# A two-layer decoder on one core: five norm tiles on GpSimd and three on VectorE, three heads' parts in flight in the last output projection, and the first key operands of the first cross-attention loaded one stage earlier

## The reference, cut to what matters

```
def _layernorm(x):  m, v = mean(x), var(x);  return (x - m) / sqrt(v + 1e-5)

layer 0:  x += self_attention(norm(x))                 # 16 heads of 32, with RoPE
          x += cross_attention(norm(x), ctx)           # 16 heads of 32; x and the weights wq, wp are
                                                       # rounded to int8 steps per row; k, v = ctx @ wkv.T + b
          x += experts(norm(x))                        # 8 experts, best 2 of them
layer 1:  x += self_attention(norm(x))
          x += cross_attention(norm(x), ctx)           # 16 heads of 128, 257 image rows apart
          x += experts(norm(x))                        # 32 experts, best 6, and shared ones
```

## Time and profile before

| what | value |
|---|---|
| median of 3 runs | 3031.25 us (3029.53 to 3034.3) |
| profiled execution, its own time | 3030.65 us |
| its span in the trace | 3028.9 us |
| TensorE busy | 2720.8 us, 90% of the span |
| mean granted TensorE clock | 0.943 of full speed |

### The profile page before, as it was taken

One profiled execution on the slowest core, in us unless ns is written; L12 is line 12 of the kernel. 1 busy time (PEld: TensorE's weight loads), 2 busy tenths in 40 slices (PEclk: granted clock), 3 DMA queues, 4 the chain that ended last, 5 costly groups with the idle time before them and its releaser, 6 DMA issues. The chain is left out here.

```text
span 3028.9 us, 47591 instructions
## 1 busy us (share of the span) xinstructions
PE 2720.8 (90%) x15710; PEld 1997.4 (66%) x15710; DVE 1479.3 (49%) x2648; ACT 1297.8 (43%) x2923; POOL 1139.0 (38%) x1037
## 2 busy tenths in 40 slices
PE   7887898996599498889999989999999879999997
PEld 5653443443588375568888879999987547777762
DVE  5575436766211427588875346767663341111115
ACT  2462524554111136466653248888872202222220
POOL 2352225666111206335554545555551302122116
PEclk9899999998699799999999999999999789999998
DMA  2332424310499414156667754444431129999987
GB/s 94 78 90 90 155 86 101 70 33 20 150 323 320 151 42 100 28 196 237 236 245 222 225 200 176 183 183 183 176 122 59 48 89 339 333 345 344 336 267 213
DMA packets 318192, 521.87 MB, mean 172 GB/s; under 512 B 35538, under 2 KB 168530, under 8 KB 309876
## 3 DMA queue, kind: packets, MB, share of 16 engines
q1 hardware_dynamic: 290100, 450.00, 46.1%
q0 software_dynamic: 13280, 43.53, 4.5%
q10 hardware_dynamic: 14688, 26.75, 2.5%
HBM read 365.39 MB, written 129.50 MB: 163 GB/s over the span
## 5 line engine op out<-in xcount | busy, mean ns | idle before, releaser
L1841 PE MATMUL ps<-moe_blocks_xgt,moe_blocks_w 128*128 128x128 f32 (+1 forms) x3000 | 357.9, 278 | 6.8 <-DMA moe_blocks_b1s<-rb_cols 3.4
L1841 PEld LDWEIGHTS ps<-moe_blocks_xgt,moe_blocks_w 128*128 128x128 f32 (+1 forms) x3000 | 342.8, 185 | 14.6 <-issue 8.5
L2804 POOL TENSOR_TENSOR normed<-normed,xa_core_rinv 128x257 f32<-128x257 f32 (+1 forms) x256 | 260.4, 1039 | 213.9 <-DVE xa_core_rinv L2728 213.9
L1912 DVE COPY moe_blocks_y<-ps 128x512 f32<-128x512 f32 x102 | 70.6, 692 | 452.6 <-PE ps L1823 452.6
L1823 PE MATMUL ps<-moe_blocks_w,moe_blocks_ht 128*128 128x512 f32 (+1 forms) x612 | 279.4, 593 | 0.0
L631 POOL TENSOR_TENSOR sa_w<-sa_w,sa_core_rinv 128x256 f32<-128x256 f32 (+3 forms) x128 | 159.2, 1253 | 223.9 <-DVE sa_core_rinv L578 223.9
L1788 POOL COPY moe_blocks_idx<-moe_index 128x1 uint32 (+1 forms) x102 | 18.7, 183 | 522.8 <-PE ps L1814 430.4
L2784 ACT ACTIVATE normed<-normed,xa_core_nmax,xa_rq 128x257 f32<-128x257 f32 (+1 forms) x256 | 206.7, 809 | 4.2
L2403 POOL TENSOR_TENSOR normed<-normed 128x512 f32<-128x512 f32 x96 | 150.6, 1569 | 116.1 <-DVE normed L2356 116.1
L1862 ACT ACTIVATE moe_blocks_xgt<-ps 128x512 f32<-128x512 f32 x102 | 60.9, 597 | 298.9 <-PE ps L1814 298.9
L868 DVE TENSOR_REDUCE xa_nmax<-ps 128x1 f32<-128x1024 f32 x128 | 149.2, 1217 | 57.8 <-PE ps L859 57.8
(11 more groups left out here) (353 smaller groups left out, 6632.8 us busy)
## 6 DMA issues: line engine op xcount, KB each, us to landing
moe_blocks_w<-L_ffn_rw SPq DMA_DIRECT2D x79, 704.0 KB
moe_blocks_w<-L_ffn_rw SPq DMA_DIRECT2D x79, 512.0 KB
k_parts<-xa_parts SPq DMA_DIRECT2D x64, 512.0 KB
v_parts<-xa_v_parts SPq DMA_DIRECT2D x128, 256.0 KB, 2.8
xa_parts<-k_parts SPq DMA_DIRECT2D x32, 1024.0 KB
xa_core_v<-v_parts SPq DMA_DIRECT2D x32, 1024.0 KB
moe_blocks_w<-L_ffn_w SPq DMA_DIRECT2D x23, 1408.0 KB
moe_y<-moe_blocks_y ACTq DMA_DIRECT2D x102, 256.0 KB
```

Source lines behind the costliest of these rows:

```text
L1841: mm = nc.tensor.matmul(g.ps[0:fn, 2 + s % 2 + 2 * half, f * P:(f + 1) * P], w1s[s][:, k, half * F + f0:half * F + f0 + fn], xgt[:, s % 2, ...
L2804: ins = nc.gpsimd.tensor_tensor(prob[:, n % PR, lo:hi], prob[:, n % PR, lo:hi], rinv[:, n % PR, m:m + 1].to_broadcast([P, hi - lo]), ALU.mult)
```

## The change

Three edits. First, NextNorm gives POOL the tiles 0 to 4 and DVE the tiles 5 to 7; DVE does them after its last reciprocal, and they count on a semaphore of their own (late). This holds at the end of both cross-attentions. Second, in output_cross1 the ring of parts has three heads; o_high and o_low lie in `parts`, and the last two heads are still taken together. Third, the key half of wkv and context chunk 0 are loaded by SP in the last stage of self-attention 0, into the two halves of g.xt, in four DMAs of 512 KB. The small norm stage at L968 is gone: DVE normalises at the head of the projection's block, into a tensor of its own, and SP issues the other seven loads there, wq now second. PE starts the keys when the two early operands are there, and waits for the value half of wkv only ahead of the values.

```diff
 class NextNorm(RowNorm):
+    POOL_TILES = 5
...
-    def normalise(self, nc, pool, t):
-        pool.wait_ge(self.rstd_done, t + 1)
-        nc.gpsimd.tensor_scalar(self.xn[:, t, :], self.g.x[:, t, :], self.g.mv[:, t, 0:1], self.g.rstd[:, t:t + 1],
-                                ALU.subtract, ALU.mult).then_inc(self.normed, 1)
+    def normalise(self, ops, eng, t):
+        eng.wait_ge(self.rstd_done, t + 1)
+        ops.tensor_scalar(self.xn[:, t, :], self.g.x[:, t, :], self.g.mv[:, t, 0:1], self.g.rstd[:, t:t + 1],
+                          ALU.subtract, ALU.mult).then_inc(self.late if t >= self.POOL_TILES else self.normed, 1)
+
+    def wait_normed(self, eng, t):
+        if t >= self.POOL_TILES:
+            eng.wait_ge(self.late, t + 1 - self.POOL_TILES)
+        else:
+            eng.wait_ge(self.normed, t + 1)
 
     def turn(self, nc, pe, t, bank):
-        pe.wait_ge(self.normed, t + 1)
+        self.wait_normed(pe, t)
...
     def store(self, sp):
         for n in range(NT // 2):
-            sp.wait_ge(self.normed, 2 * n + 2)
+            self.wait_normed(sp, 2 * n)
+            self.wait_normed(sp, 2 * n + 1)
...
-def self_attention(nc, g, name, wqkv, wo, rope, mask):
+def self_attention(nc, g, name, wqkv, wo, rope, mask, ahead=None):
...
             with nc.Block() as block:
+                if ahead is not None:
+                    @block.sync
+                    def _(sp):
+                        ahead.load(sp)
...
+class FirstKeys:
+    def __init__(self, nc, g, name, ctxt, wkvt):
+        halves = g.xt[:, :, :].rearrange("p (a k) n -> p a (k n)", a=2)
+        self.w, self.ctx = [halves[:, n, :].rearrange("p (k n) -> p k n", k=KC) for n in range(2)]
+        self.src = [wkvt[:, 0:D], ctxt[:, 0:512]]
+        self.w_loaded, self.ctx_loaded = [nc.alloc_semaphore(f"{name}_{what}_ahead") for what in ("w", "ctx")]
+
+    def load(self, sp):
+        for k in range(0, KC, 2):
+            for dst, src, sem in ((self.w, self.src[0], self.w_loaded), (self.ctx, self.src[1], self.ctx_loaded)):
+                sp.dma_start(dst[:, k:k + 2, :], src[k * P:(k + 2) * P, :].rearrange("(k p) n -> p k n", p=P)
+                             ).then_inc(sem, 16)
...
 def project_cross0(...):
-    wkv = st.sbuf("wkv", [P, KC, 2 * D])
-    ctx = st.sbuf("ctx", [P, RING, KC, 512])
+    xn = st.sbuf("xn", [P, NT, D])
+    wk, wv = first_keys.w, st.sbuf("wv", [P, KC, D])
+    ctx = [first_keys.ctx, st.sbuf("ctx1", [P, KC, 512])[:, :, :]]
...
     def load_first(sp):
-        sp.dma_start(wkv[:, :, 0:D], wkvt[:, 0:D].rearrange("(k p) n -> p k n", p=P)).then_inc(wkv_loaded, 16)
-        load_chunk(sp, 0)
         sp.dma_start(bks[:, :], bk_cols).then_inc(b_loaded, 16)
+        sp.dma_start(w_rows[0][:, :, :], wq.rearrange("(c p) n -> p c n", p=P)).then_inc(w_loaded[0], 16)
         sp.dma_start(bqs[:, :], bq_cols).then_inc(b_loaded, 16)
         sp.dma_start(bv[:, :], bkv[D:2 * D].partition_broadcast(P)).then_inc(b_loaded, 16)
-        sp.dma_start(wkv[:, :, D:2 * D], wkvt[:, D:2 * D].rearrange("(k p) n -> p k n", p=P)).then_inc(wkv_loaded, 16)
-        for n, src in enumerate((wq, wp)):
-            sp.dma_start(w_rows[n][:, :, :], src.rearrange("(c p) n -> p c n", p=P)).then_inc(w_loaded[n], 16)
         load_chunk(sp, 1)
-
-    layer_norm(nc, g, st.name + "_ln", turn=False, prefetch=load_first)
+        sp.dma_start(wv[:, :, :], wkvt[:, D:2 * D].rearrange("(k p) n -> p k n", p=P)).then_inc(wv_loaded, 16)
+        sp.dma_start(w_rows[1][:, :, :], wp.rearrange("(c p) n -> p c n", p=P)).then_inc(w_loaded[1], 16)
...
+            load_first(sp)
             for n in range(EARLY):
                 for c in range(KC):
                     store_key(KC * n + c, n, c)
...
+            for t in range(NT):
+                nc.vector.tensor_scalar(xn[:, t, :], g.x[:, t, :], g.mv[:, t, 0:1], g.rstd[:, t:t + 1],
+                                        ALU.subtract, ALU.mult).then_inc(normed, 1)
             dve.wait_ge(b_loaded, 48)
...
-            pe.wait_ge(wkv_loaded, 32)
+            pe.wait_ge(first_keys.w_loaded, 32)
+            pe.wait_ge(ctx_loaded[0], 32)
             for n in range(EARLY):
-                pe.wait_ge(ctx_loaded[n % RING], 16)
+                if n == 1:
+                    pe.wait_ge(ctx_loaded[1], 16)
...
             pe.wait_ge(row_done, 2)
+            pe.wait_ge(wv_loaded, 16)
...
 (output_cross0 and output_cross1, both)
-            for t in range(NT):
-                rn.normalise(nc, pool, t)
+            for t in range(rn.POOL_TILES):
+                rn.normalise(nc.gpsimd, pool, t)
...
             rn.invert(nc, dve, NT - 1)
+            for t in range(rn.POOL_TILES, NT):
+                rn.normalise(nc.vector, dve, t)
...
 def output_cross1(nc, g, st, a, ot, parts, rows_dram, load):
-    RING, HL = 2, 4
+    RING, HL, LAST = 3, 4, 2
     wo, bo = st.sbuf("wo", [P, H, D]), st.sbuf("bo", [P, D])
     w_high, w_low = st.sbuf("w_high", [P, RING, D], F32R), st.sbuf("w_low", [P, RING, D], F32R)
-    o_high, o_low = st.sbuf("o_high", [P, RING, B, S], F32R), st.sbuf("o_low", [P, RING, B, S], F32R)
+    o_high, o_low = [parts[:, RING * part:RING * (part + 1), :, :] for part in range(2)]
...
-            for h in range(H - RING):
+            for h in range(H - LAST):
...
-                for h in range(H - RING, H):
+                for h in range(H - LAST, H):
...
+        first = FirstKeys(nc, g, "xa0", a["ctxt"], a["wkvt0"])
+        self_attention(nc, g, "sa0", a["wqkv0"], a["wo0"], (a["cos"], a["sin"], a["swap"]), a["mask"], first)
```

More of the change, by code:

```diff
@@ L107, in __init__ @@
         self.normed, self.turned, self.copied = st.sem("rows_normed"), st.sem("rows_turned"), st.sem("rows_copied")
[L108 to L113 removed]
+        self.rows_stored, self.late = st.sem("rows_stored"), st.sem("rows_late")
+    def normalise(self, ops, eng, t):
[7 more added lines that the diff above has]
+            eng.wait_ge(self.normed, t + 1)
     def turn(self, nc, pe, t, bank):
[L116 removed]
+        self.wait_normed(pe, t)
         for k in range(KC):
@@ L886, in low_row, with cross_attention0 @@
                                 self.rows[:, i % 2, 0, :], ALU.subtract).then_inc(self.row_low, 1)
-def cross_attention0(nc, g, name, ctxt, wq, bq_cols, wkvt, bk_cols, bkv, wp, bp, rows_dram, load):
-    xn = g.xt[:, :, :].rearrange("p k (a d) -> p (k a) d", d=D)
+class FirstKeys:
[9 more added lines that the diff above has]
+                             ).then_inc(sem, 16)
+def cross_attention0(nc, g, name, ctxt, wq, bq_cols, wkvt, bk_cols, bkv, wp, bp, first, rows_dram, load):
     NKT = CTX // P
     with Stage(nc, name) as st:
+        st.sems += [first.w_loaded, first.ctx_loaded]
         ot = st.sbuf("ot", [P, B * KC, S])
@@ L900, in cross_attention0 @@
         with Stage(nc, name + "_proj") as pr:
-            project_cross0(nc, g, pr, xn, ctxt, wq, bq_cols, wkvt, bk_cols, bkv, wp, ot, packs, v, wpt, wp_scale)
+            project_cross0(nc, g, pr, first, ctxt, wq, bq_cols, wkvt, bk_cols, bkv, wp, ot, packs, v, wpt, wp_scale)
         with Stage(nc, name + "_core") as co:
@@ L937, in project_cross0 @@
     w_loaded = [st.sem("wq_loaded"), st.sem("wp_loaded")]
-    wkv_loaded, b_loaded = st.sem("wkv_loaded"), st.sem("b_loaded")
-    ctx_loaded = [st.sem(f"ctx_loaded{n}") for n in range(RING)]
+    wv_loaded, b_loaded, normed = st.sem("wv_loaded"), st.sem("b_loaded"), st.sem("normed")
+    ctx_loaded = [first_keys.ctx_loaded, st.sem("ctx1_loaded")]
     tops, scaled, inverted, shifted, clipped = (st.sem("tops"), st.sem("scaled"), st.sem("inverted"),
@@ L1045, in _ @@
             nc.vector.tensor_copy(wq_scale[:, :], scale[:, 0:KC]).then_inc(bias_done, 1)
+            dve.wait_ge(normed, NT)
             round_rows(KC, NT, 1)
@@ L1147, in key @@
                 for k in range(KC):
-                    mm = nc.tensor.matmul(g.ps[:, m % 4, :], wkv[:, k, c * P:(c + 1) * P], ctx[:, n % RING, k, :],
+                    mm = nc.tensor.matmul(g.ps[:, m % 4, :], wk[:, k, c * P:(c + 1) * P], ctx[n % RING][:, k, :],
                                           start=(k == 0), stop=(k == KC - 1))
@@ L1156, in value @@
                 for k in range(KC):
-                    mm = nc.tensor.matmul(g.ps[:, 4 + m % 2, :], ctx[:, n % RING, k, t * P:(t + 1) * P],
-                                          wkv[:, k, D:2 * D], start=(k == 0), stop=(k == KC - 1))
+                    mm = nc.tensor.matmul(g.ps[:, 4 + m % 2, :], ctx[n % RING][:, k, t * P:(t + 1) * P],
+                                          wv[:, k, :], start=(k == 0), stop=(k == KC - 1))
                 mm.then_inc(v_made, 1)
@@ L2062, in cross_attention1, with output_cross1 @@
         with Stage(nc, name + "_out") as ou:
-            output_cross1(nc, g, ou, a, ot, rows_dram, load)
-def output_cross1(nc, g, st, a, ot, rows_dram, load):
-    RING, HL = 2, 4
+            output_cross1(nc, g, ou, a, ot, parts, rows_dram, load)
+def output_cross1(nc, g, st, a, ot, parts, rows_dram, load):
```

(5 more changed lines are left out.)

8 lines of the change are left out of this document (3 added, 5 removed).

## The result

| | before | after |
|---|---|---|
| median of the runs taken together | 3032.78 us (3029.53 to 3037.53, 4 runs) | 3013.13 us (3008.21 to 3017.26, 4 runs) |
| ratio, 95% interval | | 0.9931 [0.9915, 0.9948] |
| profiled execution, span | 3030.65, 3028.9 | 3017.26, 3015.5 |

The kernel is 19.65 us faster; 22.2 was forecast. The median of after is 4.6 us above the forecast of 3008.5, inside its range. Of that, 2.1 is that before itself ran 2.1 us above the profiled execution from which the sum started (3032.78 against 3030.65).

The account below looks back on a forecast made before the run. TensorE was busy 90% of the span, so time could be won only where it waits or is slow; 11.9 + 1.8 + 8.5 = 22.2 us off 3030.65 gave 3008.5 us, range 3003 to 3018.

Parts of the forecast that it names:

- Keys ahead (11.9): Handover to cross-attention 0: early operands and no norm stage move PE's first key from 294.61 to about 282.7, 11.9 us.
- half clock included, as assumed: First keys of the projection: 3.4 us at about half clock, costing 2.0 us, were assumed to stay.
- the rival that the rounding takes over (3.6): Projection: rounding by ACT and DVE starts later relative to PE and costs 3.6 us, total 3012.1; chance 0.12.
- the forecast's own sign of being wrong: Projection, after the keys: PE idle at the first turn until ACT's integers would show the forecast wrong.
- The loss that was put at 0: Projection: loss from the rounding's later start behind PE's first key, taken as 0, with 3.6 us as other end.
- the fitted loads: Loads at the handover: landing = 282.6 + 3.1 + MB / 0.383; in the new order bv lands at 289.1.
- its own landing near 298: Projection: the first unit's store lands near 298 behind seven loads; ACT's third copy about 5 us late, costing nothing.
- Norms at cross-attention 0 (1.8): End of cross-attention 0: five norms on POOL, three on DVE gain 1.8 us, bounds 1.2 and 2.3.
- End of cross-attention 1 (8.5): Three-head ring and shared norms end the norms at 2371.7 instead of 2380.67: 9.0, less 0.46 for stores, 8.5 us.
- A dead ring: End of cross-attention 1: the ring gives nothing, PE still waits for another input; price 4.2, total 3012.7; chance 0.05.
- nothing from the keys: Projection bound further on, so early keys only wait longer; price 11.9, total 3020.4; chance 0.05.
- eight groups at half clock: Projection's keys: PE held at 1.2 GHz for all eight groups loses 25.5 us, total 3034; chance 0.03.

Follow-up runs that it names:

- keys_only: The change with only its early key loads (norm stage gone); all eight norms on POOL, ring of two heads: 3024.29 us, 0.997 of before.
- whole_again: The changed kernel unchanged, run and profiled a second time: 3016.87 us, 0.9941 of before.
- warm_values: The changed kernel plus three unread 512-column matmuls in PE's pause between the second and third value group: 3015.51 us (one run).
- ring_only: The kernel before with only the ring of three heads in the last output projection: 3028.48 us, 0.9975 of before.
- split_only: The kernel before with only the norms split, five on POOL and three on DVE, at both places: 3030.08 us, 0.9979 of before.
- wq_late: The changed kernel with the load of wq moved from second place to behind wv, the value half: 3021.03 us (one run).
- round_early: The changed kernel with biases loaded ahead of wq and POOL's memset of the ones moved behind the q units: 3014.71 us (one run).
- loads_late: The changed kernel with the value half of wkv and wp issued after the stores of the fourth key unit: 3018.39 us.
- final: Changed kernel with unread matmuls twice, biases before wq, six POOL norms at cross-attention 0, value half and wp behind eight key units' stores, earlier maxima, later memset: 3012.05 us.

## Why the prediction was right

**Keys ahead (11.9).** The first key moved from 12.12 us after the opening to 0.27: 11.85. All eight groups kept that (first turn 41.32 to 29.48), half clock included, as assumed. Up to here the forecast holds to 0.1 us. At the last integers the gain was 11.04: of the rival that the rounding takes over (3.6), 0.8 is real, 3.41 us of waiting against 2.60, and 3.39 to 3.40 in keys_only and whole_again (4.49 in warm_values). That is the forecast's own sign of being wrong (PE idle at the first turn until ACT's integers), present already before and 0.8 us larger. The loss that was put at 0 is thus 0.8. What can have made it: the landing of bv at 7.5 us after the opening (6.6 by the fitted loads), for which DVE's rounding and, unnoticed in the forecast, also ACT's first copy wait; and ACT's third copy, late by the store, at 17.1 us instead of some 12.5. The forecast called this 5 us late, which is what it was, though its own landing near 298 gives only 3 (the copy was due at 295.0). It said that the late copy costs nothing because PE asks for it only at its seventh group. That is true for PE, but ACT has less time left. The two parts were not separated. Rounding rows held beside POOL's low parts (1.37 us for one of L1061, above) are no news: five rows of over 1 us stand ahead of the last integers in before too.

Further on the gain shrank to 8.86 at wp's integers and 8.95 at the stage's end in the first pair of profiles. This isn't a bound: over three profiles each, the handover is 198.3 us without and 185.3 with the early keys, 13.0 less. In the first pair before's own stage was the shortest of its three (195.8) and after's the longest (186.9). The stretches of low clock differ between runs of one program: behind the first keys, after had them at 34.4 to 44.6 and 61.7 to 65.1 us after the opening, whole_again at 35.4 to 42.2 alone, and that is the 2.5 us between their stages as an estimate (6.8 us more at half speed, in part while PE waited). Without the early keys, ring_only and split_only have a low stretch at 72 to 79 us that before lacks. So part of the difference between 8.9 and 13.0 is luck of the clock. What sets the place of these stretches was not settled.

**Norms at cross-attention 0 (1.8).** 1.74 in the first pair, 2.4 in split_only; these differ because DVE's last reciprocal comes at another time in each. From that reciprocal to the next opening are 7.92 us in before and 6.07 in split_only, 8.14 in keys_only and 6.23 in after: 1.85 and 1.91. By steps: between the last norm's end and the next stage's first row were 4.25 us before (764.02 to 768.27) and 4.95 now (755.09 to 760.04). Of these 0.7, the stores close together cost 0.5: the last lands 3.25 us after its issue instead of 2.79, as forecast (0.46). The other 0.2 lie behind the landing and are there in keys_only too, so they don't come from the norms.

**End of cross-attention 1 (8.5).** 8.75 in the first pair. Measured from the stage's opening, POOL starts its norms 4.61 us earlier (94.96 to 90.35; 4.2 forecast: the wait of 3.10 and the half clock gone; where the other 0.4 is from was not traced). Then DVE waits 0.31 us for POOL (0.2 taken). From the last norm to the next stage are 0.84 us more (2380.67 to 2384.81 before, 2364.99 to 2369.97 now), of which the second store's later landing is 0.5 (3.25 us from issue instead of 2.76; 0.46 taken). The other 0.3 lie between its landing and the opening (1.3 us in before and ring_only, 1.6 in split_only and after), a term that the forecast didn't have. It came out right because this term and the start of POOL's norms were off by some tenths in opposite directions.

**The rivals.** A dead ring (output 1 at 110.9 alone rules it out), nothing from the keys, and eight groups at half clock did not come: the first 3.4 us ran at 0.56, the keys behind them at 1.00.

**The total.** The stage gains of the first pair are 8.9 + 1.7 + 8.8 = 19.4 us, against 19.65 between the medians. With the mean handover they would be 23.5, so the 22.2 lie between. How well 19.4 meets 19.65 is partly chance: the two profiled executions are only 13.4 us apart (3030.65 and 3017.26, the slowest of after's four), and the remaining 6 us are in stages that the change doesn't shorten.

On the rule that a ring's descriptors are consumed in ring order (the Trainium skill, DMA: Bandwidth & Descriptors, section on queues, rings and completion order): the landing of 7.3 us behind the loads, the landing at 16.4 in spite of an earlier issue (wq_late, round_early), and loads_late, where the long landing moved with the loads, agree. The forecast said that the trace before has no store behind open loads; its slowest one (2.7 us) is such a store, behind one load. On who blocks whom at the SBUF ports (the Trainium skill, SBUF — State Buffer, section on who interferes with whom): the norms of 6.93 us beside the memset and the 1.75 beside POOL's fifth norm agree with it for tensor_scalar.

## What to carry over

An early start is worth its full length only until the next engine that had been hidden by the late one; here that was ACT's and DVE's rounding, and it kept 0.8 of 11.9 us. Ask which stores stand behind a long load: two long loads put in the middle of the stores (loads_late) only chose another copy to wait. Behind all the early key stores (final) the stage was the shortest seen, but the total wasn't shown to gain. When the last two stores of a stage become ready close together, the second waits for the first; a split that lets them come 1.6 us apart and not 0.9 was worth 0.9 us, with the norm that DVE no longer does. And where untouched stages scatter by more than the edit is worth, compare the stage from barrier to barrier in several profiles, and not the totals.

## What was not expected of the hardware

- Five small matmuls whose result nobody reads, ahead of a barrier, gave PE full clock (1.00, not 0.57) in the first 4 us after it, as its idle time fell from 3.53 to 1.41 us. All four kernels that have them show no low stretch in the first keys, and all seven profiles of the change's kind without them show one of 3.4 us. It was worth 1.64 us in the keys and nothing in the end.
- In the routing the clock was low from 0.6 us after the opening even after such a start (0.54 over 15 us, then 0.50), with PE busy for 13.36 of these 15 us.
- The same program, profiled twice (after and whole_again), had a projection stage of 155.77 and 153.25 us; the last integers came at 32.87 and 32.89, and the whole difference arose behind them.
